# One opening block for loading, modulation and attention's weights, in a two-layer transformer kernel

## The reference

```python
mod = (_silu(L0_c) @ L0_wmod).reshape(L0_c.shape[0], 6, 1, -1)
sa, ca, ga, sb, cb, gb = (mod[:, 0], mod[:, 1], mod[:, 2], mod[:, 3], mod[:, 4], mod[:, 5])
ga = (2 * (ga >= 0) - 1) * jnp.maximum(jnp.abs(ga), 0.25)
gb = (2 * (gb >= 0) - 1) * jnp.maximum(jnp.abs(gb), 0.25)
h = _layernorm(x, axis=-1) * (1 + ca) + sa
x = x + ga * _L0_attn_ref(h, ...)     # 16 heads of 8, keys and values through down and up products, rotary positions
h = _layernorm(x, axis=-1) * (1 + cb) + sb
x = x + gb * _L0_ffn_ref(h, ...)      # 8 experts, the best two of each token
...                                   # layer 1: a two-way state-space mixer with a Fourier layer, then 8 experts
```

## Time and profile before

| | |
|---|---|
| median of three runs | 3375.64 us (3373.69 to 3388.64) |
| the profiled execution | 3375.44 us, its span 3373.6 us |
| busy in the span | PE 2750.7, DVE 2511.4, ACT 2260.7, POOL 2148.3 us |
| instructions in the span | 55587 |

### The profile page before, as it was taken

How to read it: one execution, slowest core, us unless ns; L and a number is a source line. 1 busy time by engine, 2 the same in 40 slices (tenths; PEclk the granted TensorE clock), 3 DMA queues, 4 the chain that set the end, 5 groups by cost and what they waited for, 6 DMA issues and landing times. The chain is left out here.

```text
span 3373.6 us, 55587 instructions
## 1 busy us (share of the span) xinstructions
PE 2750.7 (82%) x18699; PEld 2112.3 (63%) x18699; DVE 2511.4 (74%) x3291; ACT 2260.7 (67%) x4081; POOL 2148.3 (64%) x1488
## 2 busy tenths in 40 slices
PE   3999999522799996788898888888888888769984
PEld 2455555321699983466666666666666666659984
DVE  3788888534233334699999999999999999977893
ACT  1577777521222224989999998999989989756652
POOL 1223322266233333989999899998989999843564
PEclk9899999755899998989999999999999999889995
DMA  4455555221556555322222222222222222322322
GB/s 104 92 101 104 104 104 101 55 62 52 166 190 195 192 155 181 105 75 78 76 71 83 76 77 83 75 70 83 78 78 80 77 71 82 103 57 68 85 54 69
DMA packets 202031, 321.54 MB, mean 95 GB/s; under 512 B 37434, under 2 KB 108630, under 8 KB 197146
## 3 DMA queue, kind: packets, MB, share of 16 engines
q1 hardware_dynamic: 188530, 299.01, 32.0%
q0 software_dynamic: 12224, 18.29, 1.6%
q10 hardware_dynamic: 1008, 0.72, 0.1%
HBM read 269.84 MB, written 55.68 MB: 96 GB/s over the span
## 5 line engine op out<-in xcount | busy, mean ns | idle before, releaser
L1636 POOL TENSOR_TENSOR resid_x<-s_ux,s_B_rows 128x1024 f32<-128x1024 f32 x256 | 605.8, 2367 | 122.4 <-PE s_y L2357 121.3
L2188 DVE TENSOR_TENSOR_SCAN resid_x<-s_dA,resid_x 128x1024 f32<-128x1024 f32 x256 | 582.2, 2274 | 50.9 <-ACT s_dA L1848 49.6
L2196 DVE TENSOR_TENSOR_SCAN resid_x<-s_late,s_back_in 128x1024 f32<-128x1024 f32 x256 | 583.9, 2281 | 5.3 <-PE s_back_in L2344 2.9
L2357 PE MATMUL s_y<-identity,resid_x 128*128 128x128 f32 x4096 | 564.0, 283 | 8.3 <-issue 5.3
L2357 PEld LDWEIGHTS s_y<-identity,resid_x 128*128 128x128 f32 x4096 | 503.4, 147 | 61.3 <-issue 36.0
L1644 POOL TENSOR_TENSOR resid_x<-resid_x,s_C_rows 128x1024 f32<-128x1024 f32 x192 | 454.8, 2369 | 3.6 <-DVE resid_x L2188 3.4
L2203 DVE TENSOR_TENSOR resid_x<-resid_x,s_C 128x1024 f32<-128x1024 f32 x320 | 383.0, 1197 | 31.2 <-PE s_C L2332 31.2
L491 DVE TENSOR_REDUCE a_row_max<-a_maxscores 128x2 f32<-128x512 f32 x512 | 336.0, 685 | 86.0 <-PE a_maxscores L566 85.5
L1848 ACT ACTIVATE s_dA<-s_dt,s_A 128x510 f32<-128x510 f32 x512 | 330.2, 676 | 76.8 <-DVE resid_x L2188 75.6
L2344 PE MATMUL s_back_in<-identity,resid_x 128*128 128x128 f32 x2048 | 297.5, 292 | 99.4 <-ACT resid_x L1869 50.7
L1858 ACT ACTIVATE s_late<-s_dt,s_A 128x510 f32<-128x510 f32 x512 | 338.2, 710 | 0.8 <-DVE resid_x L2196 0.8
(11 more groups left out here) (449 smaller groups left out, 5588.9 us busy)
## 6 DMA issues: line engine op xcount, KB each, us to landing
s_B_rows<-forward_rows SPq DMA_DIRECT2D x256, 256.0 KB, 3.3
e_w<-L_ffn_w_by_expert SPq DMA_DIRECT2D x71, 768.0 KB, 4.6
s_C_rows<-forward_rows SPq DMA_DIRECT2D x192, 256.0 KB, 3.3
a_Q<-split_qk SPq DMA_DIRECT2D x96, 192.0 KB
split_qk<-a_parts SPq DMA_DIRECT2D x32, 384.0 KB, 2.7
e_x<-slot_inputs SPq DMA_DIRECT2D x71, 130.0 KB
a_K<-split_qk SPq DMA_DIRECT2D x64, 128.0 KB
s_late<-choice_outputs SPq DMA_DIRECT2D x16, 512.0 KB, 5.4
```

Source lines behind the costliest of these rows:

```text
L1636: tt(R[s, 0], ux[par][:], brow[s % BRING][:].unsqueeze(1).broadcast_to([P, C2, W]), ALU.mult).then_inc(S["in_ready"], 1)
L2188: nc.vector.tensor_tensor_scan(r, a, r, 0.0, ALU.mult, ALU.add).then_inc(S["scanned"], 1)
L2196: nc.vector.tensor_tensor_scan(r[:, ::-1], a[:, ::-1], b[:, ::-1], 0.0, ALU.mult, ALU.add).then_inc(S["scanned"], 1)
L2357: last = mm(YP[:, t, c2 * P:(c2 + 1) * P], R[s, d][:, c2, t * P:(t + 1) * P], core.ident[:], is_transpose=True, start=((s, d) == (0, 1) an ...
```

## The change

One block takes the place of the first two and of the opening of the third. In it:

- SP loads c, the modulation weights and the identity, then x in three lots of 8, 28 and 28 tiles (`LOTS`) with attention's weights between the first and the second and the K tiles' constant rows between the second and the third. ACT issues its seven weight loads ahead of Silu. POOL sets V and the constants from the start.
- PE makes the columns of layer 0, transposes attention's down weights, makes the columns of layer 1, the weight products, then the modulation rows and the output bias.
- DVE computes statistics and the normalisation of the first 8 tiles only, between its copies. The inverse root is Exp of -0.5 Ln on ACT, with a table set that has both loaded right behind Silu. ACT copies the modulation rows out of PSUM.

In attention's turns:

- At the start DVE finishes the rows (six instructions), SP stores them, and turn 5's gate load waits for the store.
- In turns 0 and 1 DVE computes the statistics of the second and third lot, 28 tiles each, behind L521; in turn 1 also the variance chain for the 56 tiles (`spread`). In turn 2 ACT takes Ln and Exp and DVE the product. Turn 4's normalisation is the first to need them.

The K and V tiles, the constants and the rows are allocated outside attention now and handed over as `kept`.

```diff
+LOTS = ((0, 8), (8, 36), (36, 64))
+REST = (8, 64)
+def spread(core, chain, lot, done):
+    mean, dmean, var, _ = (t[:, lot[0]:lot[1]] for t in core.ln_tmp)
+    st, tt = core.st[:, lot[0]:lot[1], :], core.nc.vector.tensor_tensor
+    chain.step(tt(mean, st[:, :, 1], st[:, :, 4], ALU.add))
+    tt(dmean, st[:, :, 1], st[:, :, 4], ALU.subtract)
+    chain.step(tt(var, st[:, :, 2], st[:, :, 5], ALU.add))
+    chain.step(tt(dmean, dmean, dmean, ALU.mult))
+    chain.step(core.nc.vector.tensor_scalar(dmean, dmean, 0.25, LN_EPS, ALU.mult, ALU.add))
+    core.nc.vector.scalar_tensor_tensor(out=var, in0=var, scalar=1.0 / D, in1=dmean, op0=ALU.mult, op1=ALU.add).then_inc(done, 1)
+def inverse_root(core, act, lot, ready, logged, done, count):
+    var, std = (core.ln_tmp[k][:, lot[0]:lot[1]] for k in (2, 3))
+    act.wait_ge(ready, count)
+    core.nc.scalar.activation(std, var, ACT.Ln).then_inc(logged, 1)
+    act.wait_ge(logged, count)
+    core.nc.scalar.activation(core.rstd[:, lot[0]:lot[1]], std, ACT.Exp, scale=-0.5).then_inc(done, 1)
...
             @block.sync
             def _(sp):
...
                 sp.dma_start(core.ident[:], aps["ident"]).then_inc(s_in, 16)
-                for k in range(LOTS):
...
-                sp.wait_ge(s_rows, 1)
-                sp.dma_start(core.modrow.rearrange("k b d -> b k d"), rows[:]).then_inc(s_out, 16)
-                sp.wait_ge(s_out, 16)
+                load_x(sp, 0)
+                for t, n in ((w_dk, "L0_attn_w_dk_by_dim"), (w_dv, "L0_attn_w_dv_by_dim"), (w_uk, "L0_attn_w_uk_by_dim"), (w_uv, "L0_attn_w_uv")):
+                    sp.dma_start(t[:], aps[n]).then_inc(S["w_loaded"], 16)
...
+                load_x(sp, 1)
+                sp.wait_ge(S["const_ready"], 1)
+                for n in range(RING):
...
+                    sp.dma_start(kept["K9"][n][KROWS:KROWS + 2, :, :], minus[:].rearrange("p (h t) -> p h t", t=T)).then_inc(S["mrow_const"], 16)
+                load_x(sp, 2)
+                sp.wait_ge(S["mrow_const"], 16 * RING)
...
             @block.scalar
             def _(act):
+                for t, n in ((w_uvg, "L0_attn_w_uv_by_group"), (w_o, "L0_attn_w_o_by_group"), (rot, "rope_rot")):
+                    act.dma_start(t[:], aps[n]).then_inc(S["w_loaded"], 16)
+                for t, n in ((cos, "rope_cos"), (sin, "rope_sin")):
+                    for k in range(2):
+                        act.dma_start(t[:, k * T:(k + 1) * T], aps[n]).then_inc(S["w_loaded"], 16)
                 act.wait_ge(s_in, 80)
                 nc.scalar.activation(cs[:], c[:], ACT.Silu).then_inc(s_silu, 1)
+                nc.scalar.preload_act_table_set(EXP_TABLE)
+                inverse_root(core, act, LOTS[0], S["var"], S["ln"], S["std"], 1)
+                act.wait_ge(s_mm, 1)
+                flat = rows[:].rearrange("b k d -> b (k d)")
+                for k, n in enumerate((512, 512, 256)):
+                    last = nc.scalar.activation(flat[:, 512 * k:512 * k + n], psR[0:B, k, 0:n], ACT.Copy)
...
             @block.tensor
             def _(pe):
...
+                columns(0)
+                pe.wait_ge(S["w_loaded"], 16 * 16)
+                for k, t in enumerate((w_dk, w_dv)):
+                    last = nc.tensor.transpose(PP[:, k * D:(k + 1) * D], t[:], core.ident[:])
+                last.then_inc(S["down_ps"], 1)
+                columns(1)
+                pe.wait_ge(S["down_T"], 1)
+                mm(PP[:, 0:D], down_T[:, 0:D], w_uk[:], start=True, stop=True)
...
             @block.vector
             def _(dve):
...
                 nc.vector.tensor_copy(cT[:], psT[:, 0:2 * B]).then_inc(s_cT, 1)
-                dve.wait_ge(s_mm, 1)
+                dve.wait_ge(s_x[0], 16)
+                for t in range(*LOTS[0]):
+                    last = nc.vector.bn_stats(core.st[:, t, :], core.X[:, t * D:(t + 1) * D])
+                chain.step(last)
+                spread(core, chain, LOTS[0], S["var"])
+                dve.wait_ge(S["down_ps"], 1)
+                nc.vector.tensor_copy(down_T[:], PP[:, 0:2 * D]).then_inc(S["down_T"], 1)
+                dve.wait_ge(s_cols, 2)
                 chain.step(nc.vector.tensor_copy(core.mod[:], psC[:, 0:12 * B]))
...
-def attention(core):
+def attention(core, kept):
...
             @block.sync
             def _(sp):
...
+                sp.wait_ge(S["modrows_ready"], 2)
+                sp.dma_start(core.modrow.rearrange("k b d -> b k d"), mod_rows[:]).then_inc(S["modrows_stored"], 16)
...
                     exponentials(i, 3)
+                    if i == 2:
+                        inverse_root(core, act, REST, S["lot_var"], S["lot_ln"], S["lot_std"], 1)
                     if i + 1 < B:
                         normed(i + 1)
...
+                nc.vector.tensor_scalar(scales, scales, 1.0, None, ALU.add).then_inc(S["modrows_ready"], 1)
+                chain.step(nc.vector.tensor_scalar(sgn[:], gates, 0.0, None, ALU.is_ge))
+                chain.step(nc.vector.tensor_scalar(sgn[:], sgn[:], 2.0, -1.0, ALU.mult, ALU.add))
+                chain.step(nc.vector.scalar_tensor_tensor(out=gates, in0=gates, scalar=-1.0, in1=gates, op0=ALU.mult, op1=ALU.max))
+                chain.step(nc.vector.tensor_scalar(gates, gates, 0.25, None, ALU.max))
+                tt(gates, gates, sgn[:], ALU.mult).then_inc(S["modrows_ready"], 1)
...
+                    if i in (0, 1):
+                        lot_stats(i + 1)
+                    if i == 1:
+                        spread(core, chain, REST, S["lot_var"])
+                    if i == 2:
+                        dve.wait_ge(S["lot_std"], 1)
+                        nc.vector.scalar_tensor_tensor(out=core.nmr[:, REST[0]:REST[1]], in0=core.ln_tmp[0][:, REST[0]:REST[1]], scalar=-0.5,
+                                                       in1=core.rstd[:, REST[0]:REST[1]], op0=ALU.mult, op1=ALU.mult).then_inc(S["rest_done"], 1)
                     row_max(i, 10)
...
-        load_and_modulate(core)
-        norm_stats(core, "lnA")
-        attention(core)
+        first = ExitStack()
+        with first:
+            attention(core, load_and_modulate(core, first))
```

More of the change, by code:

```diff
@@ new lines, in inverse_root, with offsets @@
+def inverse_root(core, act, lot, ready, logged, done, count):
[4 more added lines that the diff above has]
+    core.nc.scalar.activation(core.rstd[:, lot[0]:lot[1]], std, ACT.Exp, scale=-0.5).then_inc(done, 1)
+def offsets(core, chain, lot):
+    chain.step(core.nc.vector.scalar_tensor_tensor(out=core.nmr[:, lot[0]:lot[1]], in0=core.ln_tmp[0][:, lot[0]:lot[1]], scalar=-0.5,
+                                                   in1=core.rstd[:, lot[0]:lot[1]], op0=ALU.mult, op1=ALU.mult))
@@ new lines, in _ @@
+                load_x(sp, 1)
[4 more added lines that the diff above has]
+                sp.wait_ge(S["mrow_const"], 16 * RING)
+            @block.gpsimd
+            def _(pool):
+                for n in range(VRING):
+                    last = nc.gpsimd.memset(kept["V"][n][:], 0.0)
+                last.then_inc(S["v_zero"], 1)
+                pool.wait_ge(S["v_zero"], 1)
+                for n in range(VRING):
+                    for k in range(2):
+                        nc.gpsimd.memset(kept["V"][n][:].rearrange("p k q (a c) m -> p (k q a) c m", c=2)[:, :, k, 16 * k + DH:16 * k + DH + 1], 1.0)
+                nc.gpsimd.memset(minus[:], -1.0)
+                nc.gpsimd.memset(ones1[:], 1.0).then_inc(S["const_ready"], 1)
@@ L141, in _, with columns @@
                 pe.wait_ge(s_cT, 1)
-                for l in range(2):
+                def columns(l):
                     for k in range(6):
                         o = (l * 6 + k) * B
-                        nc.tensor.matmul(psC[:, o:o + B], w[:, l, k * D:(k + 1) * D], cT[:, l * B:(l + 1) * B],
-                                         start=True, stop=True)
+                        last = mm(psC[:, o:o + B], w[:, l, k * D:(k + 1) * D], cT[:, l * B:(l + 1) * B], start=True, stop=True)
+                    last.then_inc(s_cols, 1)
@@ L163, in _ @@
                         nc.vector.tensor_scalar(core.mod[:, o:o + B], core.mod[:, o:o + B], 1.0, None, ALU.add)
-                chain.step(nc.vector.tensor_scalar(sgn[0:B, :], psR[0:B, 0, :], 0.0, None, ALU.is_ge))
-                chain.step(nc.vector.tensor_scalar(sgn[0:B, :], sgn[0:B, :], 2.0, -1.0, ALU.mult, ALU.add))
-                for k in range(3):
-                    pair = psR[0:B, 1 + k // 2, (k % 2) * 2 * D:(k % 2 + 1) * 2 * D]
-                    nc.vector.tensor_copy(rows[:, 4 + 2 * k, :], pair[:, 0:D])
-                    nc.vector.tensor_scalar(rows[:, 5 + 2 * k, :], pair[:, D:2 * D], 1.0, None, ALU.add)
@@ L177, in _ @@
-                for k in range(LOTS):
-                    dve.wait_ge(s_x[k], 16)
-                    for t in range(k * lot, (k + 1) * lot):
-                        last = nc.vector.bn_stats(core.st[:, t, :], core.X[:, t * D:(t + 1) * D])
-                last.then_inc(s_stats, 1)
```

(19 more changed lines are left out.)

156 lines of the change are left out of this document (63 added, 93 removed).

## The result

| | before | after |
|---|---|---|
| median, both kernels in turn on one chip | 3387.41 us (3373.69 to 3394.72, 8 runs) | 3351.2 us (3343.91 to 3363.57, 8 runs) |
| ratio | | 0.9916 [0.9894, 0.9937] |
| profiled execution, its span | 3375.44, 3373.6 us | 3343.91, 3342.0 us |
| mean granted clock over the span | 0.912 | 0.907 |

The kernel is faster by 0.84%. Of the 3375.64 us shown ahead of the prediction that is 28.4 us (21 to 36 by the interval), where 27.6 had been forecast; the two medians of the table differ by 36.2 us. The profiled pair differs by 31.6 us in its spans. The runs of the changed kernel lie in two groups, 3343.91 to 3346.38 and 3356.02 to 3363.57, four in each; the profile is one of the lower group.

The account below looks back on a forecast made before the run. The prediction took the start, where engines work one after another, as the place to price: 3375.44 - 26.7 (start) + 0.2 (turn 2) - 1.1 (table load) = 3347.8, forecast 3348 us, range 3337 to 3358.

Parts of the forecast that it names:

- the work laid into the turns: Attention's turns 0 to 2: gate rows and both statistics lots covered, turn 1 by only 2.0 us; turn 2 adds 0.2 us.
- the time line to the first transpose: Start to attention's first transpose (L618): at 27.9 us instead of 54.62, 26.7 us saved; bounds 24.1 and about 29.5.
- the clock term: Granted clock in the turns' fill, 90 to 125 us: no sign, up to 10 us won or lost.
- PE's first half: Opening block on PE, from Silu through layer 0 columns, weight transposes and layer 1 columns: ends at 16.7 us.
- The first x lot: Opening block, x transfer that DVE's first statistics need: landed at 13.9 us, bounds 8.6 and 15.
- the rivals in which the transfers hold it: Opening block: transfers hold its end to 28 us, first transpose at 29.7, time 3349.6 us; 10 in 100.
- the start is not shortened: Rival at the start: something unseen gates attention's first turn, time 3370 to 3376 us; 2 in 100.
- The rival in which DVE loses its cover: Attention's turns 1 or 2: laid-in statistics delay them in full, 12.6 us, time 3360 us; 6 in 100.
- The table load: ACT's load at 106.11 us, before attention's first Exp, goes: counted as -1.1 us, at most -2.5.
- The wrong-table rival: Attention on ACT: preloaded set does not serve its mix, two reloads per turn, 82 us, time 3430 us; 2 in 100.
- the prediction's rule: Fill from 90 to 125 us: about 20 us of PE's work ran at half speed; at full speed that is 10 us.

## What the prediction had right, and which steps failed

The mechanism was right: the time follows the first transpose, and the work laid into the turns is covered. Two steps failed. The largest term of the sum, the time line to the first transpose, was mis-sized: 31.0 us saved and not 26.7. And the clock term was looked for in the fill from 90 to 125 us alone: not in turns 0 and 1, where the products were slow in before already, and not in attention's last turns, from where the 12 us come that carry a run to the end of the range and past it. In the profiled pair the 31.6 us are 31.0 at the start, 1.3 lost by the last Exp (0.9 gained in the forecast) and 1.9 gained behind attention.

**The time line to the first transpose** was 4.3 us too long (27.9 forecast, 23.62 measured, 0.5 us ahead of its lower bound). By its own parts:

1. Silu at 8.06 us, where I took the upper end, 9.6, out of 6.57 to 9.6. The shared transfers cost 1.3 us (Silu at 6.73 with the loads late; 0.2 to 1.9 over the profiles), so the nearer choice would have been the middle.
2. PE's first half was right but for that: 1.05 us from Silu to the products (1.04), columns 2.77 (2.67), weights seen at 12.09 (12.7), without a real wait.
3. The first x lot was seen at 10.54 us, not at 13.9. I had carried over the landing of a lot of twice the size. So DVE was not last; the weight products waited for PE's own columns and started at 14.99, 2.5 us early. By the forecast's own sums 0.8 of it, down to PE's 16.7, is the lot, and 1.5 is Silu.
4. Weight products 1.78 us (1.8 forecast). The 20 row products took 3.46, not 4.48, and the bias chain ended 1.67 us behind them instead of 2.4. I had taken both prices from products at half the rate. The rate doubled while the row products ran (below). PE and DVE with the bias chain were last in the block, as forecast, and the rivals in which the transfers hold it, or the start is not shortened, did not come.

These are 2.5 + 1.0 + 0.7 + 0.1 us, the 4.3. The rate shows in the windows of the row products alone; the first two rows are the changed kernel, the third is the one with all statistics in the opening, where the 20 took 4.47 us (busy PE, PEld, ACT, granted clock, transfer share, GB/s; the counts include products cut by an edge):

```profile
17.00:19.00 2.00, 2.00 (x11) 1.63 (x10) 0.00 (x0) 1.00 0.73 178
19.20:20.20 1.00, 1.00 (x10) 0.76 (x7) 0.00 (x0) 1.00 1.03 260
19.20:20.20 1.00, 1.00 (x7) 0.82 (x6) 0.00 (x0) 1.00 0.95 276
```

From one product to the next it is 0.213 us up to 18.9 us and 0.109 from 19.1 us on; in before, and in the third row's kernel, all 20 come at 0.213. The recorded clock is 1.00 in each of these rows, so at the start it cannot be read as the rate.

**What was laid into the turns** was covered, by the 2.0 us forecast (2.27 measured); the doubled statistics show that this room is the whole of it, and the opening block with all statistics that they would have cost about 14 us in front. The rival in which DVE loses its cover is answered by both.

**The table load** went as forecast, with one load (L215) for Ln and Exp. The -1.1 us counted for it is 1.4 us where it can be measured alone, from split copy to Exp. The 1.08 us of the earlier trace rows behind it is the wait of PE's weight load, not of its product, which waited 0.67. The wrong-table rival fell: there is none in attention.

**The clock term** was right to have no sign and was looked for in too narrow a place. From first transpose to first Exp the recorded clock went from 0.94 to 0.53. By the prediction's rule, half of PE's busy time at the lower level, that would cost about 13 us (an estimate from the two windows above). The stretch grew by 0.9 us, and it was 51.1 us in the second profile of the same kernel (51.9 had been forecast). Far less slow work came on top than the record says, since turns 0 and 1 were slow in before at a recorded 1.00. The larger piece lay where I had not looked, in attention's last turns, where a wait for one element's K tiles was followed by a loss of 12 to 23 us. The medians of the changed kernel, 3351.2 and 3358.79 us, are mixtures of its two groups, and so are those of before. The agreement of 28.4 with 27.6 us is therefore partly luck: the start gave 4 us more, and the rest depends on how many runs of each group were drawn on either side. In the lower group the time is 3344 to 3348 us, in the upper one 3356 to 3364, the end of the range and past it. Stages after attention changed by -1.9 us, as nothing should touch them; in the other profiles they took 2749.3 to 2755.9 us, so that is scatter.

## What to carry to other kernels

Work that stands alone at a start can be laid into the first turns of a pipeline at no cost as far as the waits of its engine reach there, and the width of that cover can be read from one row; take it for the limit. When a load is split or shared, size its landing by its own bytes and not by the landing of the larger one before. Where runs of one program lie in two groups, compare the profile of one execution from each before crediting an edit: here the clock behind a single wait at the end of a stage cost 12 us and more, over a third of what the start saved. And take the rate of products from their spacing where the recorded clock has not yet changed.

## What the hardware showed that I had not expected

- One PE wait of 1.6 to 2.2 us in a stretch that is busy before and after it was followed, in four profiles, by a granted clock of 0.50 for some 24 to 55 us, while PE stayed busy; products came at about half the rate (56 in 10 us against 104). Waits of 1.1 to 1.8 us in other executions of near-identical code had no such effect.
- A recorded clock of 1.00 did not mean full rate at the start of a program: row products came every 0.213 us up to 18.9 us and every 0.109 from 19.1 us on, at 1.00 on both sides, and in before a rotary product took 2.04 us at 59 us and 1.10 at 87.5, again at 1.00.
- Loads of 0.72 MB whose last issue came 6.0 us later had moved about 7 us later (by 17 us instead of 10), with 1.8 MB of x beside them in place of the modulation inputs.
